# Two attention stages on one core: the products with V in one block per job, not in two halves

## The reference, cut to what matters

```python
# layer 0: 16 heads of 16, keys no further than 128 from the query
energy = einsum('bhqd,bhkd->bhqk', q, k)
energy = where(abs(i_q - i_k) > 128, fmin, energy)
out = einsum('bhqk,bhkd->bhqd', softmax(energy / 16), v)

# layer 1: blocks of 64. Query blocks first and last see all keys; block 1 sees 0, 1, 2, last;
# the last but one sees 0 and the last three; a block n between them sees 0, n-1, n, n+1 and last.
out = einsum('bhqk,bhkd->bhqd', softmax(scores / 4), v)
```

## Time and profile before

| | us |
|---|---|
| median of 3 runs | 2486.34 |
| profiled execution | 2498.06 |
| its span, first to last instruction | 2496.3 |
| TensorE / VectorE / ScalarE / GpSimd busy in the span | 2221.6 / 1841.6 / 1663.3 / 1066.3 |
| VectorE: reductions of stage 0 (L667, x1024) | 472.7 |
| VectorE: reductions of stage 1 (L672, x1152) | 566.6 |
| ScalarE: exponentials (L720, x2176) | 908.6 |
| TensorE: products with V (L816, x10496) | 562.7 |

### The profile page before, as it was taken

The page is one execution under the profiler, slowest core; times in us unless marked ns, Lnnn a source line. Parts: engine busy times, 40 slices in busy tenths (PEclk is TensorE's granted clock), DMA queues, the critical chain, the costliest instruction groups (busy, mean ns, idle before and its releaser), DMA issues. The chain is left out here.

```text
span 2496.3 us, 73453 instructions
## 1 busy us (share of the span) xinstructions
PE 2221.6 (89%) x25549; PEld 1349.1 (54%) x25549; DVE 1841.6 (74%) x5599; ACT 1663.3 (67%) x3892; POOL 1066.3 (43%) x1370
## 2 busy tenths in 40 slices
PE   7979999999976788859999995986999999999775
PEld 4643444444344566748888884553344444544354
DVE  5549999999646677735454454775999999999297
ACT  7946888889923555415454453874599999999643
POOL 3533555555568466626666663543000000000075
PEclk9987999999988899979999997997799999999878
DMA  7552333333231566635554344675233333322242
GB/s 232 188 186 66 90 97 89 92 91 92 52 114 56 135 185 184 166 94 125 141 128 105 93 92 126 209 258 194 51 79 77 78 79 76 81 75 65 77 138 86
DMA packets 363698, 289.66 MB, mean 116 GB/s; under 512 B 228400, under 2 KB 296752, under 8 KB 363344
## 3 DMA queue, kind: packets, MB, share of 16 engines
q1 hardware_dynamic: 349616, 248.24, 37.3%
q0 software_dynamic: 12960, 35.60, 4.5%
q10 hardware_dynamic: 768, 1.12, 0.2%
HBM read 133.53 MB, written 123.69 MB: 103 GB/s over the span
## 5 line engine op out<-in xcount | busy, mean ns | idle before, releaser
L720 ACT ACTIVATE a_pr<-a_pst 128x384 f32<-128x384 f32 (+3 forms) x2176 | 908.6, 486 | 117.8 <-PE a_pst L755 81.4
L755 PE MATMUL a_psc<-a_ke,a_qe 52*128 52x128 f16 (+5 forms) x3072 | 647.8, 290 | 34.9 <-DMA a_ke<-mrow 31.5
L672 DVE TENSOR_REDUCE a_mx<-a_psc 128x1 f32<-128x384 f32 (+2 forms) x1152 | 566.6, 563 | 19.6 <-PE a_psc L755 14.4
L755 PE MATMUL a_pst<-a_qe,a_ke 53*128 53x128 f16 (+5 forms) x3072 | 564.0, 281 | 2.8 <-ACT a_pr L720 0.2
L816 PE MATMUL a_po<-a_pr,a_ve 128*17 128x128 f32 (+3 forms) x10496 | 562.7, 302 | 2.1 <-ACT a_pr L720 1.2
L667 DVE CUSTOM_DVE_ANT_0 a_cut<-a_psc,row_mask 128x384 bf16<-128x384 f32 (+1 forms) x1024 | 472.7, 521 | 24.2 <-PE a_psc L755 12.2
L755 PEld LDWEIGHTS a_pst<-a_qe,a_ke 53*128 53x128 f16 (+1 forms) x3072 | 209.5, 94 | 331.7 <-ACT a_pr L720 187.5
L642 POOL TENSOR_SCALAR_AFFINE_SELECT a_pr<-a_pr 128x512 f32<-128x512 f32 x448 | 275.1, 634 | 205.2 <-ACT a_pr L720 205.2
L755 PEld LDWEIGHTS a_psc<-a_ke,a_qe 52*128 52x128 f16 (+1 forms) x3072 | 223.2, 94 | 145.7 <-DVE a_mx L672 44.1
L816 PEld LDWEIGHTS a_po<-a_pr,a_ve 128*17 128x17 f32 x10496 | 193.8, 96 | 191.7 <-issue 116.5
L628 POOL TENSOR_SCALAR a_mneg<-a_mx 128x32 f16<-128x32 f32 x64 | 18.4, 288 | 634.5 <-DVE a_mx L676 589.0
(11 more groups left out here) (234 smaller groups left out, 4189.6 us busy)
## 6 DMA issues: line engine op xcount, KB each, us to landing
a_qe<-qx SPq DMA_DIRECT2D x378, 64.0 KB, 2.7
a_ke<-kx SPq DMA_DIRECT2D x378, 64.0 KB, 2.7
vx<-p_vst SPq DMA_DIRECT2D x32, 544.0 KB, 3.3
a_ve<-vx SPq DMA_DIRECT2D x64, 272.0 KB, 3.2
qx<-p_stg SPq DMA_DIRECT2D x64, 256.0 KB, 3.2
kx<-p_stg SPq DMA_DIRECT2D x64, 256.0 KB, 3.1
ox<-a_ost SPq DMA_DIRECT2D x256, 64.0 KB
x_res<-x SPq DMA_DIRECT2D x16, 512.0 KB, 9.1
```

The lines of the kernel that those rows point to most:

```text
L672: dve.tensor_reduce(out.unsqueeze(1), psc[(u * n_s + n) % RING][:, 0:width], AXX, ALU.max)\
L720: act.activation(pr[s % SLOTS][:, h // 2, h % 2, 0:width], pst[prob_slot(u, n) % RING][:, 0:width], ACT.Exp, scale=scale).then_inc(p_ready, 1)
L755: last = pe.matmul(out[:, col:col + count], stat, mov(tok, count), start=(k == 0), stop=(k == len(pieces) - 1), skip_group_check=True, til ...
```

## The change

One line of `with_v`. With `middle = 0` no piece belongs to part 0, and all are in part 1. Part 0 keeps its place and its waits (V loaded, the output bank copied, the probabilities made or cut), and issues no matmul. TensorE's order in a job becomes P S P S P S P S and then the whole block of products with V, 16 or 24 instructions.

```diff
@@ -807,7 +807,7 @@
                 for tok, w, col in v_cuts(s):
                     halves = [(tok, w // 2, col), (tok + w // 2, w - w // 2, col + w // 2)] if w > 3 * 64 else [(tok, w, col)]
                     pieces += halves
-                middle = (len(pieces) + 1) // 2
+                middle = 0
                 opened = {c[0] // CH for q in range(s) for c in v_cuts(q)}
                 for n, (tok, w, col) in enumerate(pieces):
                     h = tok // CH
```

## The result

The changed kernel takes 2678.97 us (median of 4 runs, 2670.55 to 2688.81) against 2484.7: ratio 1.0777, 95% interval 1.0729 to 1.0824. It is slower, as forecast, but by 194 us and not by 98, and lies outside the range. Its profiled execution took 2670.55 us (span 2668.8).

The account below looks back on a forecast made before the run. VectorE, fed through three score banks, was taken to bound both attention stages. Longer turns of 54 and 36 us plus 8 for ScalarE's copies made 98 us, so 2584 us, 3.9% slower, range 2513 to 2615.

Parts of the forecast that it names:

- What bounds the kernel, and the turn through the ring: Both attention stages: VectorE bounds, fed through three score banks; stage 0's wide turn grows from 1.92 to 2.23 us.
- w: Turn term: from VectorE's start on a tile to the weight load three tiles on; 0.61 us for 384 columns.
- s: Turn term: from that weight load to the start of the products with V; 0.26 us.
- V: Turn term: from the products' start to the next tile's load; 0.45 us for a half, 0.77 for a 384-column block.
- r: Turn term: from a tile's weight load to VectorE's start on it; 0.59 us in stage 0, 0.42 in stage 1.
- the forecast's sum of its turns: Stage 1: the turns of a unit's nine jobs add to 19.2 us against 18.05, 36 us over 30 units.
- TensorE's clock falls: Rival, both stages: idle ahead of each job halves the granted clock to 1.2 GHz; 2800 us and up, chance 0.03.
- The wide tiles' chain through VectorE: ScalarE's output copies behind the block: VectorE's chain called longer than ScalarE's, so they were put at 8 us.
- the bound of 36: Upper bound, in us, on what ScalarE's output copies starting behind the block could cost: 0.6 x 60.
- The price of the clock's rival: Both stages at half clock: each turn's streamed columns take twice as long, some 0.5 us more for 510 jobs.
- No change: Rival: banks freed or filled some 0.3 us sooner, turns fit in VectorE's time; 2480 to 2495 us, chance 0.07.
- Faster by fewer changes: Rival: merging saves TensorE's 0.14 us a block and 0.16 idle, units fall to VectorE's need; 2440 us, chance 0.06.

Follow-up runs that it names:

- e5: One block in stage 1 alone (halves in stage 0), each stage 1 output bank copied one job later, against the kernel before: 2539.46 us, ratio 1.0213.
- e3: Changed kernel plus eight filler matmuls a job in stage 0: 2638.92, 2638.95, 2728.68 and 2777.19 us in four executions, no ratio.
- e9: Changed kernel with VectorE's score wait behind its two bookkeeping instructions in stage 0, timed again: median 2598.3 us, ratio 1.0459 to the kernel before.
- e10: Changed kernel with VectorE's score wait placed last in stage 0 and output banks copied one job later in both stages: 2553.26 us, ratio 1.0285.
- e4: Changed kernel with VectorE's reduction over at most the first 256 columns of each score tile: 2580.24 us in one execution.
- e7: One block in stage 1 alone, in the middle of the job instead of its end, against the kernel before: 2546.62 us (one execution), +59.
- e6: Opposite edit, products with V in up to three parts a job, against the kernel before: 2510.82 us, ratio 1.0091.
- e2: One block in stage 0 alone, halves in stage 1, against the kernel before: 2623.24 us, ratio 1.0525.
- e8: Changed kernel with VectorE's score wait behind its two bookkeeping instructions in stage 0, first execution: 70 us under the changed kernel.

## Why the prediction was right or wrong

- *What bounds the kernel, and the turn through the ring*: right. The terms were w 0.62, s 0.27, V 0.77, r 0.59 in stage 0 and a turn of 2.07 in stage 1, each within 0.02 us. With the copies taken out, stage 1's unit is 19.59 us (e5), 0.35 over the forecast's sum of its turns.
- *"TensorE's clock falls ... Against it: TensorE would still work some 80% of each job, and the clock stands at 1.00 with the waits of now"*: this is the step that failed most, for the sum had nothing for the clock. It was a rival at 0.03, written as if it would hold for the whole of both stages, and it came for parts of stage 0: 39 us there in the profiled execution and, by e3, some 12 of the 14.8 of that stage's tail. The other executions were slower at lower mean clocks (2688.81 us at 0.900). The argument against it doesn't carry: TensorE's share, whose ends are modelled, is 86% in the changed kernel at full clock and 84% in e9, where the clock stayed up, so in these rows it doesn't tell the two apart. And it looked at steady stretches only: in the kernel before too, the clock stands at 0.50 at the start of each stage.
- *"The wide tiles' chain through VectorE (0.59 + 0.61) is longer than the one through ScalarE, so I take near the lower end, 8 us"*: wrong, a term mis-sized. The copies behind the block cost 0.48 us a unit in stage 1 (e5) and 0.51 in stage 0 (e9 to e10, 16.28 to 15.77), 30 x 1.0 = 30 us, near the bound of 36. I had compared the chains of a job without a copy; in the job behind one ScalarE starts 0.5 us later, and its chain is the longer.
- *The price of the clock's rival*: "some 0.5 us more" for each job was 0.97 (3.22 - 2.25).
- *No change*: the ring did not cover it; e4 shows that one reduction's length goes into the turn once, and e7 that the place of the block doesn't matter.
- *Faster by fewer changes*: e6 gives its size, 0.16 us a change or somewhat more, against 0.32 us of products taken into the turn.

The sum, then, for the profiled executions: turns 64 - 15 + 61 - 14 = 96 us (forecast 90), copies 29 (8), clock 39 in stage 0 (0), the two tails 15 (12 of it the clock) + 4 (0), less 10 elsewhere: 173 against a forecast of 98. That the direction was right is no luck, since the turn that gave it was measured; but even with the copies at their bound the forecast's sum ends at 126 us, and what lies beyond it is the clock. What stays open is what decides when the clock falls: e2 and the changed kernel show it low for different stretches of the same stage, the executions of e3 differ among themselves, and all that is shown is that with a turn of 2.07 us instead of 2.25 the clock stayed up from 230 us to stage 0's last scores in the three traces of such a kernel (e8, e9, e10), and by the mean clocks in every execution of e9 and e10.

## What to carry to other kernels

Where one engine feeds another through a ring of few banks, add up one turn (read, free, the longest block between two tiles, fill, start) and compare it with what the reader needs for as many tiles as lie between two such blocks; a switch saved is worth nothing if the block grows past that. Do the same for every other ring that the block crosses, in the job where its engine has a second duty. And a pause that appears in each job may cost a second time through TensorE's clock, as it did here in parts of a stage: price that case by parts, not as all or nothing. And where a side effect of a change has been mended, compare with a kernel before that is mended in the same way: the block seemed to cost 69 us and cost 85.

## What the runs showed of the hardware that was not expected

- The same code ran from the start of stage 0 to about 446 us at the clock's lower level, with TensorE's share at 97% (e2, 300 to 400 us), and at the upper level with it at 86%: once low, the clock stayed low for over 250 us while TensorE hardly paused by a profile in which the ends of matmuls are modelled.
- Every traced kernel starts both attention stages at the lower level, the kernel before too: it leaves it at about 216 us in stage 0, the changed one at 230, and the one with the block in stage 0 alone only at 446.
- A wait that is placed ahead of two instructions without data work, instead of behind them, cost VectorE 0.18 us at each late tile, and 16 us of the kernel with halves, which had seemed to have no slack to give.
